# Five-piece weight setup, and TensorE steps of the Mamba half that may pass up to three others in the order table

## What is computed

```python
def _mamba2_block(x, ln_w, ln_b, in_proj_w, conv_w, conv_b, A_log, D, dt_bias, gamma, out_proj_w):
    u = _layernorm(x, ln_w, ln_b)                       # x: 8 x 1024 x 512
    zxbcdt = u @ in_proj_w.T                            # z 1024 | xs 1024, B 128, C 128 | dt 16
    dt = softplus(zxbcdt[..., -NHEADS:] + dt_bias)
    xBC = silu(conv4(xBC) + conv_b)                     # depthwise, 4 taps, 1280 channels
    # per head: state = state * exp(dt * A) + dt * x * B;  y = C . state + D * x
    y = y * silu(z)
    y = y * rsqrt(mean(y * y, -1) + EPS) * gamma
    return x + y @ out_proj_w.T

def _L0_ffn_ref(x, w_qr, w_kvr, w_q, w_kv, w_out, null_kv, null_token):
    # for each of 4 groups: top 512 queries and top 256 keys by a routing product,
    # gathered, 8-head attention with a null key, output projection, scattered mean
...
xn = _layernorm(x)
return x + _mamba2_block(xn, ...) + _L0_ffn_ref(xn, ...)
```

## Time and profile before

| what | us |
|---|---|
| median of three executions (3781.61 to 3785.87) | 3782.2 |
| the profiled execution | 3792.61 |
| its span, first to last instruction | 3791.2 |
| TensorE busy in the span | 3569.1 (94%) |
| VectorE busy | 2945.2 (78%) |
| ScalarE busy | 2546.7 (67%) |
| GpSimd busy | 1857.4 (49%) |

### The profile page before, as it was taken

One profiled execution on the slowest core, in us unless ns is written; L12 is line 12 of the kernel. 1 busy time (PEld: TensorE's weight loads), 2 busy tenths in 40 slices (PEclk: granted clock), 3 DMA queues, 4 the chain that ended last, 5 costly groups with the idle time before them and its releaser, 6 DMA issues.

```text
span 3791.2 us, 72352 instructions
## 1 busy us (share of the span) xinstructions
PE 3569.1 (94%) x28354; PEld 2166.4 (57%) x28354; DVE 2945.2 (78%) x5342; ACT 2546.7 (67%) x4781; POOL 1857.4 (49%) x1483
## 2 busy tenths in 40 slices
PE   4799999999999999999868999999999999999998
PEld 2455555555555555555534666556666566666665
DVE  3888898978888888888968777777777777677764
ACT  3777777777777777785536666677666766666665
POOL 0233333323333332322437878876656766666565
PEclk7899999999999999999878999999999999999999
DMA  3332333323232233322344333444333433343332
GB/s 115 83 79 68 76 77 74 81 76 90 65 71 73 76 89 77 90 65 43 67 70 130 64 76 70 80 94 95 75 78 70 109 83 70 70 81 77 73 67 38
DMA packets 297668, 294.27 MB, mean 78 GB/s; under 512 B 38663, under 2 KB 222599, under 8 KB 295280
## 3 DMA queue, kind: packets, MB, share of 16 engines
q1 hardware_dynamic: 241008, 186.70, 19.6%
q0 software_dynamic: 56320, 102.94, 15.6%
HBM read 176.19 MB, written 101.71 MB: 73 GB/s over the span
## 4 chain that ended last, share of the span: by engine, by line
PE 74%; DVE 13%; ACT 6%; issue 3%; DMA 3%; POOL 1%; SPq 0%; another core or an unknown queue 0%; DVEq 0%; ACTq 0%; POOLq 0%
PE pair L1243 9%; PE pair L1374 8%; PE pair L1289 7%; PE pair L1326 7%; PE pair L1489 6%; PE pair L1336 5%; PE pair L1389 4%; PE pair L1403 4%; PE pair L1450 3%; PE pair L1449 3%; PE pair L1419 2%; PE pair L1308 2%; PE pair L1317 2%; ACT de L2080 2%; PE pair L1470 2%
## 5 line engine op out<-in xcount | busy, mean ns | idle before, releaser
L2335 POOL TENSOR_TENSOR ph<-pf,ph 128x512 f16<-128x512 f32 x256 | 379.7, 1484 | 317.0 <-ACT ph L2195 314.1
L1635 DVE SCALAR_TENSOR_TENSOR cv<-raw,taps,cv 128x512 f32<-128x512 f32 x480 | 428.8, 904 | 63.3 <-ACT cv L2050 60.1
L1889 DVE TENSOR_REDUCE smx<-pair 128x2 f32<-128x514 f32 x512 | 350.4, 687 | 80.1 <-PE pair L1419 77.0
L1243 PE MATMUL pair<-xhT,whi 128*128 128x512 f16 x1280 | 382.4, 380 | 0.2
L2189 ACT ACTIVATE pf<-pair 128x1024 f32<-128x1024 f32 x256 | 262.3, 1025 | 96.9 <-PE pair L1450 93.0
L1289 PE MATMUL pair<-zhi,xhT 128*128 128x512 f16 x1024 | 325.4, 379 | 1.2 <-ACT ob L2112 1.2
L1326 PE MATMUL pair<-ohi,yT 128*128 128x512 f16 x1024 | 317.6, 382 | 1.1 <-ACT yT L2107 1.1
L2080 ACT ACTIVATE de<-de,cum 128x128 f32<-128x128 f32 x1024 | 311.3, 393 | 1.0
L1924 DVE TENSOR_TENSOR ph<-pf,ph 128x512 f16<-128x512 f32 x256 | 232.4, 908 | 97.9 <-ACT ph L2195 96.5
L2195 ACT CAST ph<-pf 128x1024 f16<-128x1024 f32 x256 | 268.3, 1048 | 4.4
L1336 PEld LDWEIGHTS pair<-xdt,de 128*128 128x128 f32 x2048 | 240.7, 194 | 17.3 <-issue 10.4
(11 more groups left out here) (272 smaller groups left out, 10487.6 us busy)
## 6 DMA issues: line engine op xcount, KB each, us to landing
de<-cum SPq DMA_DIRECT2D x64, 1024.0 KB, 9.4
rows<-rowt SPq DMA_DIRECT2D x16, 1040.0 KB, 5.4
xin<-x SPq DMA_DIRECT2D x16, 1024.0 KB, 7.2
y<-xin SPq DMA_DIRECT2D x16, 1024.0 KB, 4.5
y<-ob POOLq DMA_DIRECT2D x64, 256.0 KB, 4.3
qb<-qa SPq DMA_DIRECT2D x32, 512.0 KB
rbc<-rank SPq DMA_DIRECT2D x63, 256.0 KB
wst<-wkv SPq DMA_DIRECT2D x32, 256.0 KB
```

What stands on the lines that cost most here:

```text
L1243: ins = pe.matmul(bk[:], w[:, k, ws], xt[:, ha, k, :], start=n == 0, stop=n == 3 * KD - 1)
L1635: ve.scalar_tensor_tensor(c_[:], r_[:, t:t + BLK], taps[:, ct, t:t + 1], c_[:], ALU.mult, ALU.add).then_inc(done, 1)
L1889: ve.tensor_reduce(smx[:, qt, 2 * h2:2 * h2 + 2], sc[:, :, 0:NK + 1], AX.X, ALU.max)
L2335: po.tensor_tensor(p_[:, 1, 1], f[:, 1], p_[:, 0, 1], ALU.subtract).then_inc(S.plp, 1)
```

## The change

It changes the setup, and the order of the Mamba half.

- `w_in` is loaded in five other pieces (`PIECES`): first the columns of convolution tiles 7 to 9 and dt, then tiles 0 to 3, tiles 4 to 6, and last z in two halves. `x_in(0)` is issued ahead of the small loads; `w_out` comes after the last piece.
- The bias products are made another way. For a piece with convolution channels `slice_bias` takes the fp32 weights themselves as the stationary operand and `ln_b` as one moving column, which puts the bias of a tile straight into one column: 12, 16 and 12 matmuls of one column, and in piece 0 also four of 16 columns for dt. Only z's pieces still use the broadcast `lb_bc`. `bias_get` takes the result out on VectorE. `bias_bc` and the ten transposes are gone.
- There is no `weights_ready`. All setup steps but the small ones (`slice_in`, `slice_high`, `slice_low`, `slice_bias`, `bias_get`, `zbias_high`, `wout_in`, `wout_high`, `wout_low`) and block 0's normalization are now steps of `Order`, and the steps that need them wait for them alone: `logits` for piece 0, `conv` for its tile's piece, `z` for its half, `proj` for `w_out`. `w_out` is loaded into the place of tiles used later, for which `z_tanh` waits.
- `Order` is run with `ahead=AHEAD_M` = 4 in the Mamba half: a step of TensorE may pass up to three others, never one of its own kind.
- Where block 1's turns and convolutions are mixed in is moved (`AHEAD_1`, `CONV_START_1`).

```diff
-AHEAD = 12
+AHEAD, AHEAD_M = 12, 4
+AHEAD_1, CONV_START_1 = (-0.06, 3.64), -0.25
-NC5 = 5
-CUTS = (0, 512, 1024, 1456, 1888, WC + NH)
+PIECES = ((DI + 7 * P, WC + NH), (DI, DI + 4 * P), (DI + 4 * P, DI + 7 * P), (0, 512), (512, DI))
+TILES = ((7, 10), (0, 4), (4, 7))
+PIECE_OF = (1, 1, 1, 1, 2, 2, 2, 0, 0, 0)
...
+    first = [("x_in", 0)]
+    alone = Order(plan.twin(), first, ahead=AHEAD_M)
...
+    order = Order(plan, first, [t for step, t in alone.at.items() if alone.nodes[step][0] == "DVE"], ("bit", "ranks", "ranks_zero"), ahead=AHEAD_M)
...
+        if name == "slice_bias":
+            add("PE", 4.9 if a > 2 else 3.5, step, [("slice_in", a)], [("single", [("bias_get", a)])])
...
+    for n in range(len(PIECES)):
+        add("SP", 0.5, ("slice_in", n), [("slice_low", n - 2), ("slice_bias", n - 2)] if n > 1 else [], extra=6.0 if n else 2.0)
+        add("ACT", 2.6 if n else 3.4, ("slice_high", n), [("slice_in", n), last(("slice_high", n - 1)) if n else None])
+        add("DVE", 2.7 if n else 3.2, ("slice_low", n), [("slice_high", n)])
...
+    record.steps += [("slice_bias", 0), ("turn", 0, 0), ("turn", 0, 1), ("turn", 0, 2), ("turn", 0, 3),
+                     ("slice_bias", 1), ("logits", 0), *(("conv", 0, ct) for ct in CONVS[:2]), ("slice_bias", 2), ("cum", 0),
+                     *(("conv", 0, ct) for ct in CONVS[2:5]), ("slice_bias", 3), *(("conv", 0, ct) for ct in CONVS[5:8]),
+                     ("slice_bias", 4), *(("conv", 0, ct) for ct in CONVS[8:]), ("z", 0, 0), ("z", 0, 1)]
...
-            def stage_(n):
+            def slice_bias(n):
+
+                s = stage[n % 2]
                 q.wait_ge(S.stage[n % 2], 16 * (n // 2 + 1))
...
+                if n < len(TILES):
+                    for m in range(TILES[n][1] - TILES[n][0]):
+                        for k in range(KD):
+                            ins = pe.matmul(bk[:, m:m + 1], s[:, k, m * P:(m + 1) * P], lb[:, k:k + 1], start=k == 0, stop=k == KD - 1)
+                    if n == 0:
+                        for k in range(KD):
+                            ins = pe.matmul(bk[:, NH:2 * NH], lb_bc[:, k, :], s[:, k, 3 * P:3 * P + NH], start=k == 0, stop=k == KD - 1)
+                else:
+                    for k in range(KD):
+                        ins = pe.matmul(bk[:], lb_bc[:, k, :], s[:, k, :], start=k == 0, stop=k == KD - 1)
                 ins.then_inc(S.wb_mm, 1)
...
-            def weights_ready():
-                q.wait_ge(S.rb, NCT)
...
             def conv(i, ct):
                 q.wait_ge(S.xT, CK * (i + 1))
+                q.wait_ge(S.wlo_m, PIECE_OF[ct] + 1)
...
+            def slice_in(n):
+                c0, c1 = PIECES[n]
                 q.wait_ge(S.wb_mm, n - 1)
                 q.wait_ge(S.wlo_m, n - 1)
+                sp.dma_start(stage[n % 2][:, :, 0:c1 - c0], wr[:, :, c0:c1]).then_inc(S.stage[n % 2], 16)
+
+            def wout_in():
+                sp.dma_start(wout_f[:], w_out.rearrange("(k p) n -> p k n", p=P)).then_inc(S.wout, 16)
```

More of the change, by code:

```diff
@@ L435, in arrange @@
 def arrange(plan, line):
-    first = [(name, 0) for name in ("x_in", "stat0", "stat1", "stat2")]
-    first += [(name, 0, c) for c in range(CK) for name in ("xn", "row_high", "xh", "row_low", "low", "skip", "turn", "turn_out")]
-    alone = Order(plan.twin(), first)
+    first = [("x_in", 0)]
+    alone = Order(plan.twin(), first, ahead=AHEAD_M)
     arrange_steps(alone, [step for step in line if step[0] not in ("rank_in", "slots", "row")], False)
     alone.run()
-    order = Order(plan, first, [t for step, t in alone.at.items() if alone.nodes[step][0] == "DVE"], ("bit", "ranks", "ranks_zero"))
+    order = Order(plan, first, [t for step, t in alone.at.items() if alone.nodes[step][0] == "DVE"], ("bit", "ranks", "ranks_zero"), ahead=AHEAD_M)
     arrange_steps(order, line, True)
@@ L462, in arrange_steps @@
         name, a, b = (*step, 0, 0)[:3]
-        if name == "turn":
+        if name == "slice_bias":
+            add("PE", 4.9 if a > 2 else 3.5, step, [("slice_in", a)], [("single", [("bias_get", a)])])
+        elif name == "turn":
             add("PE", 0.45, step, [("low", a, b)], [("single", [("turn_out", a, b)])])
         elif name == "logits":
-            add("PE", 1.33, step, [("turn_out", a, c) for c in range(CK)], [("single", [("logits_out", a)])])
+            add("PE", 1.33, step, [("turn_out", a, c) for c in range(CK)] + [("slice_low", 0)], [("single", [("logits_out", a)])])
         elif name == "cum":
@@ L469, in arrange_steps @@
         elif name == "conv":
-            add("PE", 2.6, step, [("turn_out", a, CK - 1)], [("single", [("raw", a, b)])])
+            add("PE", 2.6, step, [("turn_out", a, CK - 1), ("slice_low", PIECE_OF[b])], [("single", [("raw", a, b)])])
         elif name == "gram":
@@ L476, in arrange_steps @@
         elif name == "z":
-            add("PE", 3.02, step, [("turn_out", a // CK, CK - 1)], [("single", [("z_silu", a, b)])])
+            add("PE", 3.02, step, [("turn_out", a // CK, CK - 1), ("slice_low", 3 + b), ("bias_get", 3 + b)], [("single", [("z_silu", a, b)])])
         elif name == "gate":
@@ L484, in arrange_steps @@
         elif name == "proj":
-            add("PE", 5.18, step, [("gate_out", a)], [("single", [("proj_out", a)])])
+            add("PE", 5.18, step, [("gate_out", a), ("wout_low", KI - 1)], [("single", [("proj_out", a)])])
         elif name == "rank_in":
@@ new lines, in arrange_steps @@
+        seen = [("low", i - 1, CK - 1), ("skip", i - 1, CK - 1)] if i else []
+        add("DVE", 3.2, ("stat0", i), [("x_in", i)] + seen)
+        add("POOL", 1.5, ("pow1", i), [("stat0", i)])
+        add("DVE", 1.2, ("stat1", i), [("pow1", i)])
+        add("POOL", 1.5, ("pow2", i), [("stat1", i)])
+        add("DVE", 0.25, ("stat2", i), [("pow2", i), last(("logits_out", i - 1))])
+        for c in range(CK):
+            before = (i, c - 1) if c else (i - 1, CK - 1)
+            two = (i, c - 2) if c > 1 else (i - 1, CK - 2 + c)
+            add("ACT", 0.81, ("xn", i, c), [("stat2", i)] + [last((name, *before)) for name in ("low", "row_low", "xh")])
+            add("ACT", 0.62, ("row_high", i, c), [("xn", i, c), last(("rows_out", i - 1))])
+            add("ACT", 0.72, ("xh", i, c), [("xn", i, c), last(("turn", *two))])
+            add("POOL", 1.3, ("row_low", i, c), [("row_high", i, c)])
+            add("DVE", 0.9, ("low", i, c), [("xh", i, c)])
+            add("ACT", 0.81, ("skip", i, c), [("xn", i, c)])
+            add("ACT", 0.58, ("turn_out", i, c), [("turn", i, c)] + [last(("z", CK * (i - 2) + CK - 1, 1))])
@@ L774, in back @@
             yield 0.9
+    plan.append(("x_in", 0))
     plan.append(("prep",))
[L777 to L787 removed]
     plan.settle()
     record = Record()
[L791 to L794 removed]
+    record.steps += [("slice_bias", 0), ("turn", 0, 0), ("turn", 0, 1), ("turn", 0, 2), ("turn", 0, 3),
+                     ("slice_bias", 1), ("logits", 0), *(("conv", 0, ct) for ct in CONVS[:2]), ("slice_bias", 2), ("cum", 0),
+                     *(("conv", 0, ct) for ct in CONVS[2:5]), ("slice_bias", 3), *(("conv", 0, ct) for ct in CONVS[5:8]),
+                     ("slice_bias", 4), *(("conv", 0, ct) for ct in CONVS[8:]), ("z", 0, 0), ("z", 0, 1)]
     ahead = Feed(turns(1), TURNS, record)
@@ L1134, in program @@
         psum = {
-            "stage": lambda n: [(S.wb, n + 1)],
-            "bias": lambda: [(S.rb, c + 1) for c in range(NCT)],
+            "slice_bias": lambda n: [(S.rb, n + 1)],
             "turn": lambda i, c: [(S.xT, CK * i + c + 1)],
```

199 lines of the change are left out of this document (82 added, 117 removed).

## The result

The changed kernel takes 3759.6 us (median of 5 runs, 3752.5 to 3764.1) against 3782.4 for the kernel before (5 runs, 3781.6 to 3785.9): a ratio of 0.9935, 95% interval 0.9922 to 0.9948. It is 23 us faster. The forecast was 71 us and the range ended at 3742, so the forecast is wrong: the sign was right, a third of the size came.

The account below looks back on a forecast made before the run. TensorE, busy 94% of the span, was taken to bound most of the kernel, VectorE the end of the Mamba half. Terms 40 + 22 + 9 = 71 us took 3782.2 to 3711; range 3684 to 3742.

Parts of the forecast that it names:

- Term A: Setup up to `open(0)`: `open(0)` 37.6 us earlier plus 2.8 for z done ahead; 40 us gained, between 30 and 50.
- term B: TensorE's waits from 160 to 1720 us, mostly gates for `y_low` with low clock behind: 22 us gained, ends 5 and 30.
- Slower: Rival: z steps passing `intra` and `gate` hold banks, so pairs are missing in each of 63 chunks; 3796 us, 3%.
- Only the setup pays: Rival: waits of 2 us taken from the gate show at `proj`, `intra` or a bank; 3740 us, 14%.
- Term C: From `cum(15)` to attention: its bank wait goes and the tail waits less; 9 us gained, ends -4 and 18.
- The handover: Mamba half to attention, within term C: rank steps mixed with chunk 63's, first gather about 1.5 us later.

Follow-up runs that it names:

- no_passing: Against the changed kernel, TensorE goes strictly by its line in the Mamba half (AHEAD_M = 1), the five-piece setup kept; median 3764.3 us, ratio 0.9944.
- slots_first: Against the changed kernel, no passing in the Mamba half except that `slots` goes ahead of gate(63); median 3746.4 us, ratio 0.9897.
- z_in_place: Against the changed kernel, z steps may pass no other steps from chunk 4 on, all others still may; median 3730.8 us, ratio 0.9864.

## Why the prediction was wrong, point by point

*Term A, the setup: the way to `open(0)` was right.* The turns were forecast at 25, 33, 37 and 41; PE's timeline, with all of `slice_bias(1)` in the second row:

```profile
26.68 1.03 PE L1223 MATMUL pair<-id,xh 128*128 128x128 f16 x8 [4.54 <-DVE xh L1596]
27.51 6.93 PE L1209 MATMUL pair<-lb,stage 128*128 128x1 f32 x32
34.30 1.01 PE L1223 MATMUL pair<-id,xh 128*128 128x128 f16 x8
38.39 1.03 PE L1223 MATMUL pair<-id,xh 128*128 128x128 f16 x8 [3.07 <-DVE xh L1596]
41.50 1.03 PE L1223 MATMUL pair<-id,xh 128*128 128x128 f16 x8 [2.08 <-DVE xh L1596]
```

`xn(0, 0)` at 21.94 (21.5 forecast), `logits(0)` at 47.4 (47), the first convolution tile at 48.7 (49), `open(0)` at 109.0 (106; within 100 to 112). The 16 small fp32 matmuls took 6.93 us, 0.43 each where I had 0.47 from `cum`'s row; each has two records. The clock was the low one, as forecast: the turns beside them took 1.03 us, and a turn took 1.06 at 118.41, at 0.5, but 0.62 at 108.29, at 1.00. (The trace holds no clock ahead of 51.7 us, and the profile counts that time as 1.00.) The Trainium skill's 107 ns a weight load ("TensorE: Matmul & The Clock Gate", section "LDWEIGHTS (loading the stationary operand)") would have made 1.7 us of them, an estimate from that page; the measurement decides for the row.

*The step of A that failed is the one from `open(0)` to the regular work*, "`open(0)` comes 143.6 - 106 = 37.6 us earlier" and "since everything behind it is the regular Mamba work". 34.6 and the 5.6 us of z that are done ahead make 40.2; at `conv(2,0)` 27.3 are left. Behind `open(0)` the clock was at 0.5 for 27.3 us (before: until 146.5, 2.9 us). Half of the difference, some 12 us of TensorE's work, is nearly all of the 12.9; this is worked out, and what two executions of the same order show beside it is 6.5 us for 13.7 us at 0.5. The row was there: the clock of 0.81 in the first 160 us. I took it for a mark of the idle time and counted no cost where work follows it. In term B I had counted exactly this tail behind 2 us gates, and not behind waits of 5 and 4 us. Without passing, z is not ahead and `conv(1,8)`, the first tile of block 1, comes only 14 us earlier than before instead of 27: there the setup, priced at 40, was worth 21.

*Term B: the waits went where I said, and others came.* The gate waits went (15.0 to 4.1), forecast 22; measured from `conv(2,0)` to `intra(56)`: minus 19. The sentence that failed is "Steps that pass others also hold their banks earlier. I take three quarters". It is the mechanism of the rival *Slower*, which I gave 3%. I priced its turning point at 0.8 us a chunk; z steps that pass cost 5.6 us a batch, 0.7 a chunk. All other passing gains 2.5 us a batch against before (222.7 to 220.2), of which 0.9 came without any passing (221.8); beside the old setup it gains 3.1 (219.6). My arguments against it were both weak. "The plan counts all 8 banks" is true of the plan's durations, and a bank that comes free 2 us later than planned is enough. That TensorE waited for `z_silu` once before says nothing, since z passed nothing then. "Only the setup pays" comes nearest of the rivals in its number (3740, still 20 us off) but not in its reason: the setup paid half of its price, and the rest is a gain and a loss of about the same size.

*Term C was right up to `row(0,5)`*: from `intra(56)` the lead grew by 12.4, of which 5.7 by `cum(15)`, whose wait went; 9 had been forecast. But VectorE isn't above 95% busy in the tail. From 1780 to 1910, the same part of the program as 1800 to 1930 before, it is busy 119.9 of 130 us, against 122.5 in the earlier trace rows. TensorE still waits there for `y_low`, 12.2 us from 1740 to 2010 instead of 23.5 in the earlier trace rows.

*The handover, forecast at minus 1.5 within term C, gave 10 us and more*, so by the traces term C as a whole gave 24.5 us, beyond its upper end of 18. (Some of this may be the 10 us by which the traced execution of before stood above its median; where those lie isn't known.) Neither the 8.56 us of SyncE's issue nor the order of the store was among the rows that I read. I followed the moved `slots` on VectorE and not on SyncE's queue.

By ratios on 3782 us the whole reads: setup 21 (no_passing), `slots` ahead 18 (slots_first), the other passing without z 12 (z_in_place), z's passing minus 27 (the changed kernel). Each is a difference of neighbouring ratios, known to about 7 us, so that they add up to the measured 24.6 is no check of them. Only z's share was measured twice, 27 beside the new setup and 28 beside the old.

## What to carry to other kernels

When a plan lets steps overtake, ask of each kind what it holds while it waits: a step that takes a PSUM bank long before its result is wanted belongs in its place, and one kind of step can eat what all others gain. Count a lead only where the next bound begins: time won ahead of a stretch in which TensorE idles in pieces can be lost again to half clock behind it, and since two executions of one order differed there by 13.7 us of low clock, one trace doesn't settle such a loss. Of a moved step follow the transfer that it sets off, up to what is queued behind that.

## What the runs showed of the hardware

- Between bits of idle time TensorE did whole stretches of 13.7 us at 0.5 of the clock with hardly a pause in them. With 35 matmuls of 512 columns without use in 9 us of waiting, 3.4 us at 0.5 were left of 27.3 behind `open(0)` in one kernel, and 17.1 in another that differs only behind 334 us.
- With the same order on TensorE, VectorE and ScalarE, these 13.7 us more at 0.5 made the stretch of some 140 us 6.5 us longer.
- The store of the score table took 13.9 to 17.2 us from issue to landing. The issue of a load that is sent to all partitions held SyncE's queue for 8.6 to 8.8 us when it came 3.3 to 3.8 us behind this store, still under way, and 0.33 us when it came 17 us or more behind. Which resource the two share, no trace here shows.
